# A stretch between two attentions placed as guest steps into one attention of 24 items

## What is computed

```python
# L0: cross attention, 16 heads of 8, adaLN on both sides
x = x + attend(adaln(x) @ Wq, adaln(ctx) @ Wkv) @ Wp
# L1: one head of 128 over the context, then experts
nx = layer_norm(x)
weights = softmax((nx @ Wq) @ (ctx @ Wk).T * 128**-0.5)
evidence = weights @ (ctx @ Wv)
combined = concat(nx, evidence, cond)
probs = softmax(combined @ router_W)                    # 3 experts
routed = sum(probs[e] * (silu(combined @ e_w1[e]) @ e_w2[e]) for e in range(3))
x = x + sigmoid(silu(combined @ gate_w1) @ gate_w2) * (routed @ out_w)
# L2 and L3: self-attention over the 56 tokens, cross attention over the 1500 keys, MLP
x = x + gate_a * (attend(qkv(modulate(ln(x)))) @ W_proj)
x = x + attend(ln(x) @ W_qc, ln(ctx) @ W_kvc) @ W_cproj  # L3: context without the norm
x = x + gate_m * (gelu(modulate(ln(x)) @ W1) @ W2)
```

## Time and profile before

| | us |
|---|---|
| median of 3 runs | 888.12 |
| range of the runs | 883.29 to 888.56 |
| the profiled execution's own time | 883.98 |
| its span | 882.2 |
| first copy of an item's output (L726) | at 89.9 |
| end of a0: last output copy | at 248.96 |
| first output copy of a1 | at 466.97 |
| last output copy | at 857.0 |

### The profile page before, as it was taken

How to read it: one execution, slowest core, us unless ns; L and a number is a source line. 1 busy time by engine, 2 the same in 40 slices (tenths; PEclk the granted TensorE clock), 3 DMA queues, 4 the chain that set the end, 5 groups by cost and what they waited for, 6 DMA issues and landing times.

```text
span 882.2 us, 23060 instructions
## 1 busy us (share of the span) xinstructions
PE 795.9 (90%) x9613; PEld 534.1 (61%) x9613; DVE 593.2 (67%) x1301; ACT 503.2 (57%) x786; POOL 393.2 (45%) x519
## 2 busy tenths in 40 slices
PE   6659999999989988687599999999999899999996
PEld 4336667777656634365167777767766676666763
DVE  7947877777623266454667777876778768777834
ACT  8337777776612220343077776666667656666663
POOL 7764766663000500752856666752335505333000
PEclk9689999999999999898689999999999999999999
DMA  8795545436935200440924454433452443543200
GB/s 213 195 232 124 139 112 141 133 91 199 316 118 161 65 20 1 142 108 15 223 63 130 126 141 125 122 89 108 135 162 83 130 131 89 156 130 97 57 3 10
DMA packets 82171, 106.71 MB, mean 121 GB/s; under 512 B 11502, under 2 KB 75758, under 8 KB 81812
## 3 DMA queue, kind: packets, MB, share of 16 engines
q1 hardware_dynamic: 81492, 104.62, 43.2%
q10 hardware_dynamic: 576, 0.63, 0.3%
HBM read 41.37 MB, written 0.23 MB: 47 GB/s over the span
## 4 chain that ended last, share of the span: by engine, by line
PE 72%; DVE 14%; POOL 6%; ACT 4%; issue 2%; DMA 2%; SPq 0%; DVEq 0%; POOLq 0%; ACTq 0%
PE ring_ps L589 14%; PE oacc_ps L614 14%; PE score_ps L603 12%; PE ring_ps L573 7%; PE ring_ps L566 6%; DVE max_sb L707 4%; PE ring_ps L559 3%; PE ring_ps L1644 2%; DMA kstack<-part_sb 2%; DVE tok L1411 1%; PE score_ps L1491 1%; PE ring_ps L579 1%; POOL hat_sb L773 1%; POOL kstack L2002 1%; ACT prob_sb L686 1%
## 5 line engine op out<-in xcount | busy, mean ns | idle before, releaser
L707 DVE TENSOR_REDUCE max_sb<-ring_ps 128x1 f32<-128x500 f32 x576 | 365.9, 672 | 104.0 <-PE ring_ps L589 101.6
L686 ACT ACTIVATE prob_sb<-score_ps 125x896 f32<-125x896 f32 x288 | 255.3, 921 | 85.3 <-PE score_ps L603 84.7
L589 PE MATMUL ring_ps<-kstack,qstack 128*128 128x500 bf16 x576 | 200.4, 391 | 25.9 <-DMA kstack<-part_sb 11.1
L782 POOL TENSOR_TENSOR key_sb<-key_sb,part_sb 128x500 f32<-128x500 f32 x72 | 82.0, 1140 | 189.5 <-ACT key_sb L668 188.9
L603 PEld LDWEIGHTS score_ps<-qstack,kstack 128*128 128x128 bf16 (+1 forms) x2304 | 139.2, 102 | 42.8 <-issue 11.7
L603 PE MATMUL score_ps<-qstack,kstack 128*128 128x112 bf16 (+1 forms) x2304 | 158.2, 215 | 3.1 <-ACT prob_sb L686 2.3
L614 PE MATMUL oacc_ps<-prob_sb,val_sb 125*32 125x168 f32 (+1 forms) x3456 | 139.5, 294 | 0.9 <-ACT prob_sb L686 0.6
L614 PEld LDWEIGHTS oacc_ps<-prob_sb,val_sb 125*32 125x32 f32 x3456 | 97.5, 109 | 49.0 <-issue 19.6
L589 PEld LDWEIGHTS ring_ps<-kstack,qstack 128*128 128x128 bf16 x576 | 51.1, 99 | 90.3 <-DVE max_sb L707 33.6
L787 POOL TENSOR_TENSOR part_sb<-key_sb,part_sb 128x500 bf16<-128x500 f32 x72 | 82.5, 1146 | 5.6
L773 POOL TENSOR_SCALAR hat_sb<-nat_sb,norm_now 125x128 f32<-125x128 f32 x184 | 81.4, 459 | 1.7
(11 more groups left out here) (301 smaller groups left out, 1003.2 us busy)
## 6 DMA issues: line engine op xcount, KB each, us to landing
kstack<-part_sb SPq DMA_DIRECT2D x432, 125.0 KB, 2.4
nat_sb<-ctx_nat SPq DMA_DIRECT2D x20, 672.0 KB
qstack<-qpart_sb SPq DMA_DIRECT2D x60, 112.0 KB, 2.3
nat_sb<-ctx_T SPq DMA_DIRECT2D x8, 750.0 KB, 4.4
w_sb<-ctx_nat SPq DMA_DIRECT2D x5, 672.0 KB
w_sb<-weights SPq DMA_DIRECT2D x1, 3268.5 KB, 13.5
kstack<-ctx_T SPq DMA_DIRECT2D x4, 750.0 KB, 13.7
nat_sb<-ctx_nat SPq DMA_DIRECT2D x20, 78.0 KB
```

The source lines that it names most:

```text
L589: last = pe.matmul(ps[:, 0:KB], queries(p, n, D), kstack[:, u, p, j * KB:(j + 1) * KB], start=True, stop=True)
L686: return act.activation(dst, score_ps[0:CK, c % 2, :, 0:HALF], ACT.Exp)
L707: return dve.tensor_reduce(max_sb[:, p, j:j + 1], ring_ps[:, self.bank[f"{i}.{name}"], 0:KB], AX.X, ALU.max)
L782: return pool.tensor_tensor(rest, rest, part_sb[:, 0, cols], ALU.subtract)
```

## The change

There is one `Attention`, "att", of 24 items (L0, L2, L3 with 8 each). The stretch is gone. A new class `First`, derived from `Half`, does for one half what the stretch did: its HEAD steps (L0's projection, all of L1) and then the own part that `Half` already had (L2's self-attention, projection and cross queries). Guest e0a (batches 0 to 3) stands in periods 4 to 6, e0b in periods 8 to 10, each with its last steps of GpSimd and SyncE in the period after (e0b's of VectorE, too). L2's items 8 to 15 follow item 7 with no break, so items 8 and 12 wait for the queries that e0a and e0b make. A guest `pre` (class `Before`) has the modulation products (period 0), the load of the weights of L1 and L2 (3076.5 KB, SyncE, period 3) and the anchor products (TensorE, period 3, behind S1). The third layer group's guests move by 8 periods: e2a to 12 to 14, e2b to 16 to 18, e3a and e3b to 21 to 24. `keep_busy` fillers of the stretch, `Dense` d1, d2 and d_mid, `Evidence` and `Own` are removed; `L2_W_proj` has one block of 128 columns instead of four.

The evidence is computed for two batches at a time, in thirds of 500 keys. The context for it is no longer held whole: it comes through two buffers `ev_in`, in twelve steps c0 to c11 per half, each of two transfers of 250 KB; step c(i) waits for the TensorE step that used c(i-2). The scores are copied by ScalarE into `ev_sc`.

```diff
+GUESTS = {'e0a': {...
+         ('pe', 4): 'proj:M0.2 e.mean:K0 e.var:PV0 e.rep:K1 eq:S5 eqk:M1.2 s00:M1.3 s01:PV2 s02:M1.7 pt00:PV4 pt01:PV4 '
+                    'u00:M2.7 pt02:M2.7 u01:M2.7 u02:MTb s10:V2 ut0:V2',
...
+         ('sp', 5): 'c5:load c6:load c7:load c8:load c9:load c10:load c11:s0.0',
...
-        d1 = Dense("d1", [("proj", "dve", "x"), *L.ln_products("ln"), ("q", "dve", "q"), ("qk", "dve", "qk")],
-                   [], ["x", *L.ln_values("ln"), "nx", "q", "qk", "anchors"])
-        evi = Evidence()
...
-        own2 = Own("own2", w("L2_W_qkv", 0, 256, 128), vec("L2_b_qkv", 2))
...
-        a0 = Attention("att0", [(layer0, n) for n in range(B)], EARLY_L0, {})
-        a1 = Attention("att1", [(l, n) for l in (layer2, layer3) for n in range(B)], EARLY_L2,
-                       {B: next_queries(halves[0]), B + HB: next_queries(halves[1])}, halves, BANKS)
...
+        guests = [before, e0a, e0b, e2a, e2b, e3a, e3b]
+        a0 = Attention("att", [(l, n) for l in (layer0, layer2, layer3) for n in range(B)], EARLY_L0,
+                       {B + HB * i: next_queries(g) for i, g in enumerate((e0a, e0b, e2a, e2b))}, guests, BANKS)
...
+                ps = self.ring(pe, "anch")
+                pe.wait_ge(loaded_w1, 16)
+                for k in range(len(ANCHORED)):
+                    last = pe.matmul(ps[:, k * B:(k + 1) * B], anchored(k, 2), cond_sb[:, :], start=True, stop=True)
+                yield self.done("pe", last, "anch")
...
+                w1 = W_AT["L1_Wq"][0]
+                sp.wait_ge(stats_kept, B)
+                sp.dma_start(w_sb[:, w1:W_L3], weights[:, w1:W_L3]).then_inc(loaded_w1, 16)
+                yield "w1"
...
+            HEAD = {
+                "pe": "proj e.mean e.var e.rep eq eqk s00 s01 s02 pt00 pt01 u00 pt02 u01 u02 s10 ut0 s11 s12 pt10 pt11 u10 pt12 "
+                      "u11 u12 ut1 ev lA lB w0 g2 w1 o0 w2 o1 o2 out",
...
+                "dve": "e.x e.xc e.sq e.vs e.xh nx eqk mx0 rec0 sc0 out0 mx1 rec1 sc1 out1 l01 l2 gu m01 m d gh s01 s r pp "
+                       "u0 g u1 h0 h1 u2 x0 h2 x1 a1 x2 a2 outg x",
...
+            def evidence_scores(self, pe, k, j):
...
+                block, loaded = self.part(k, j)
+                pe.wait_ge(*loaded)
+                for t in range(2):
+                    at = (2 * k + t) * LQ
+                    last = pe.matmul(ps[64 * t:64 * t + 64, 0:KB], ev_q[:, at:at + 64], block[:, t, 0:KB], start=True, stop=True,
+                                     skip_group_check=True)
...
+            def combined(self, pe, name, ks):
+                ps = self.ring(pe, name)
+                for i, k in enumerate(ks):
+                    for c, rhs in enumerate((self.xe, self.ev)):
+                        last = pe.matmul(ps[:, i * HT:(i + 1) * HT], anchored(k, c), rhs, start=(c == 0), stop=(c == 1))
...
+            def head_sync(self, sp):
+                for index in range(12):
+                    k, i = divmod(index, 6)
+                    block, (into, _) = self.part(k, i)
+                    if index >= 2:
+                        sp.wait_ge(*self.after("pe", self.taken_in(index - 2)))
...
+                    for t in range(2):
+                        n = HB * self.h + 2 * k + t
+                        if i < NJ:
+                            sp.dma_start(block[:, t, 0:KB], ctx_T[n][:, i * KB:(i + 1) * KB]).then_inc(into, 16)
+                        else:
+                            c = 4 * (i - NJ)
+                            sp.dma_start(block[0:CK, t, :].rearrange("p (c k) -> p c k", c=4), ctx_nat[n][:, c:c + 4, :])\
+                                .then_inc(into, 16)
+                    yield f"c{index}"
```

More of the change, by code:

```diff
@@ new lines @@
+GUESTS = {'e0a': {('act', 4): 'eq:E5 c00:K2 c01:K2 c02:E7 ex0:V0 p00:E11 p01:E11 p02:E11 c10:V2 c11:V2',
[40 rows of a table added]
+         ('dve', 11): 'm.vs:O m.xh:O m.q:O m.q.0:O',
[54 rows of a table added]
+         ('dve', 23): 'e.xc:O e.sq:OTT e.vs:OTT e.xh:OTT e.scaled:OTT e.shifted:OTT',
+         ('dve', 24): 'in0:OTT in1:OTT h0:OTT h1:OTT gated:OTT x:OTT',
+         ('pe', 22): 'proj:PV5 e.mean:MTb',
+         ('pe', 23): 'e.var:S4 e.rep:S10 u0:PV5',
+         ('pe', 24): 'u1:OT y:OTT',
+         ('pool', 21): 'e.rs:k2.2',
+         ('sp', 21): 'store:s2.2'},
+ 'e3b': {('act', 23): 'u0:E11 u1:E11 sq0:E11 u2:E11 u3:E11 sq1:E11 t0:E11 t1:E11 y:E11',
+         ('dve', 24): 'e.x:OTT e.xc:OTT e.sq:OTT e.vs:OTT e.xh:OTT e.scaled:OTT e.shifted:OTT in0:OTT in1:OTT h0:OTT '
+                      'h1:OTT gated:OTT x:OTT',
+         ('pe', 24): 'proj:OTT e.mean:OTT e.var:OTT e.rep:OTT u0:OTT u1:OTT y:OTT',
+         ('pool', 21): 'e.rs:k2.2',
+         ('sp', 21): 'store:s2.2'},
+ 'pre': {('dve', 0): 'mods:M0.1 scales:M0.1',
+         ('dve', 3): 'anch:M0.1',
+         ('pe', 0): 'mods:S1',
+         ('pe', 3): 'anch:S1',
+         ('pool', 0): 'keys0:norm keys1:hat0 pads0:hat0 pads1:hat2 ones:hat2',
+         ('sp', 3): 'w1:load'}}
@@ L1068, in vector, with head_vector @@
             def vector(self, dve):
-                nm, l, h = self.nm, self.layer, self.h
+                yield from self.head_vector(dve)
+                if self.follow:
+                    yield from self.own_vector(dve)
+            def head_vector(self, dve):
+                nm, l = self.nm, self.layer
                 dve.wait_ge(*self.after("pe", "proj"))
@@ L1142, in scalar, with head_scalar @@
             def scalar(self, act):
+                yield from self.head_scalar(act)
+                if self.follow:
+                    yield from self.own_scalar(act)
+            def head_scalar(self, act):
                 nm = self.nm
@@ L1171, in scalar @@
                 act.wait_ge(*self.after("pe", "val"))
-                act.wait_ge(own_pads_ready, 3)
+                act.wait_ge(*before.after("pool", "ones"))
                 for n in range(HB):
@@ L1242, in sync @@
                     return
+                yield from self.head_sync(sp)
                 def placed(part, into):
@@ L1949, in _ @@
             sp.dma_start(x_t, x_T).then_inc(loaded_x, 16)
-            for g in halves:
+            for g in guests:
                 g.begin("sp", sp)
@@ L2130, in _ @@
-            a1.run("pe", pe, -1, only=lambda name: name[0] in "VM")
-            for p in a1.periods():
-                a1.run("pe", pe, p)
         @block.scalar
         def _(act):
-            for g in halves:
+            for g in guests:
                 g.begin("act", act)
@@ L2288, in _ @@
-            d = d2
-            dve.wait_ge(d.pe.sem, d.pe.after("ev"))
-            d.step(dve, dve.tensor_copy(ev_t, d.ps("ev")), "ev")
-            for e in range(E_N):
-                dve.wait_ge(d.pe.sem, d.pe.after(f"l{e}"))
-                d.step(dve, dve.tensor_tensor(by_batch(logit[e]), by_batch(d.ps(f"l{e}")), anchor(e), ALU.add), f"l{e}")
-            d.step(dve, dve.tensor_tensor(xc_t, logit[0], logit[1], ALU.max), "m01")
-            d.step(dve, dve.tensor_tensor(xc_t, xc_t, logit[2], ALU.max), "m")
@@ L2331, in _ @@
-            d.gated(dve, T(8), "L2.gate_a", "y")
-            d.ln_dve(dve, "ln", 1e-6)
-            dve.wait_ge(d.pe.sem, d.pe.after("q"))
-            d.step(dve, dve.tensor_scalar(q_t, d.ps("q"), vec(nm["q_b"]), HD ** -0.5, ALU.add, ALU.mult), "q")
-            d.split(dve, q_t, [qsplit_sb[:, i, :] for i in range(3)], "q")
-            for p in a1.periods(-1):
-                a1.run("dve", dve, p)
 def kernel(**inputs):
```

1045 lines of the change are left out of this document (416 added, 629 removed), and 138 rows, old and new, of tables (EARLY_L2, GUESTS, HEAD, WEIGHTS).

## The result

The changed kernel takes 910.09 us (median of 4 runs, 907.10 to 912.49), the kernel before 885.70 in the same comparison: a ratio of 1.0273, 95% interval 1.0240 to 1.0307. It is slower by 2.7%. The forecast was 860 and its range ended at 894, so neither the size nor the sign held.

The account below looks back on a forecast made before the run. TensorE bounds plain attention periods; the stretch between attentions is a dependent chain. Base 701.7, work 88.0 and 5.2, waits 5, 15, 10, 27 and 6 give a span of 857.9; plus 1.8, 860 us. Range 822 to 894.

Parts of the forecast that it names:

- e0a: First new half, periods 4 to 7: 44.0 us of TensorE work, and a wait of 8 us at its end.
- e0b: Second new half, periods 8 to 11: 44.0 us of TensorE work, and a wait of 16 us at its end.
- e2a: Guest half of the third layer group, there already: keeps its cost inside the base, 94.5 us for three periods.
- Evidence loads: New halves: TensorE waits for context steps, about 6 us at the first half's c5; 10 in all, 3 to 25.
- Rival B: Evidence transfers of 125 partitions run on 5 of 16 engines, 8 us more per half: 876 us, chance 0.22.
- The clock: Half clock behind waits: 3 us at the anchor products in period 3 and 3 after the end of the halves.
- TensorE's work: Head 29.2 and own part 14.8 us per half come back into the attention's periods: 88.0 for both halves.
- Modulation products: They move into period 0 and cost TensorE 2.8 us.
- Anchors: Period 3, behind S1: TensorE waits 12 us for the weight load, plus 3 for the clock: 15, 9 to 16.
- Half ends: Before M0.0 of periods 7 and 11: waits for queries of 8 and 16 us, 3 for the clock: 27, 17 to 33.
- VectorE's burst: M1.2 to M2.4 of periods 5 and 9: 25 guest steps make TensorE wait 3 us per half, 6 in all.
- Rival C: The evidence steps run on still fewer engines, such as three: 902 us, slower than before, chance 0.07.

Follow-up runs that it names:

- the split: The changed kernel with each 125-partition evidence transfer made two, of 112 and 13 partitions: 892.47 us, ratio 1.0090 to the kernel before.
- the reverse edit: The 868.51 us kernel with its evidence transfers whole again, 125 partitions each: 887.87 us, ratio 1.0045 to the kernel before.
- the fastest kernel: Changed kernel with evidence transfers divided, anchor and modulation products moved later, fillers ahead of items 8 and 12, c5 and c6 issued earlier: 868.51 us, ratio 0.9840.
- the fillers' periods: Periods 7 and 11 of the changed kernel with filler matmuls ahead of items 8 and 12: 907.24 us, ratio 1.0196 to the kernel before.

## Why the prediction was wrong

- **The base** (701.7 us) held as far as the table can show it: the items follow one another, and outside periods 4 to 11 the differences sum to 8.3 us.
- **Evidence loads, 10 us (wait 3): the step that failed most.** That its upper bound of 25 is what was measured is luck: it stood for twelve late landings at full width. The forecast took a 125-partition transfer to be as wide as the 128-row ones; it is a third as wide. The waits were 25.4; the split gave 17.6 us back, the reverse edit cost 19.4. Rival B had the mechanism and the price (16), and a chance of 0.22 where the rule and the 112 and 13 partitions in the natural-layout loads of before spoke for it. Its price fits in part by luck: B charged six uncovered steps, and eight waited. What B missed is that everything else in the queue has its share on the five engines, too.
- **The clock, 6 us.** I priced a wait at half clock twice (3 us at the anchors, 3 at one half end). In fact ten stretches at half clock lie in periods 4 to 11, nine of them at or just behind waits of 1.8 to 7.8 us, and they cost 19.7 us of speed where 3 were priced: two thirds of the 28 us of busy time above 194.2 + 88. Not all of it is paid: fillers in all long waits gave TensorE 17 us back, and the time fell by 4 to 9.
- **TensorE's work, 88 us (the step "work that comes back").** Without the lost speed it is 96.6 in the change, 10% more than priced; the fastest kernel gives the same (312.5 busy us, less 15.2 of fillers, 194.2 plain and 7.4 for the half clock: 96). By the lines of that kernel the evidence takes 35.7 us where 29.6 were priced, and the head's 64 dense products 32.4 where 26.2 were, 0.5 each in place of 0.41. Both prices came from rows with many like products in a row; that they cost more one by one between other products is argued, not tried.
- **Modulation products, 2.8 us.** Right at full clock (2.95), but they stood where the clock was at half, and cost 5.2. The memory sets, put at nothing as lying in the removed stretch, stood behind them on GpSimd, which waited 8.8 us.
- **Anchors, 15 us:** right; the weights landed 11.8 us after their issue (the 9 us of pure transfer in its lower bound stand in no row; at the 312 KB per us that the forecast takes elsewhere they are 9.9), period 3 was 1.6 us shorter than priced, and moving the products gave 9.8.
- **Half ends, 27 us:** waits of 6.8 and 7.8 at M0.0 with 2.7 in the chain ahead of it (mean, variance, query), and 4.6 of clock by the fillers' periods: 22, a little less than priced. From the end of V2 to M0.0 e0b's chain took 13.5 us in place of 16.
- **VectorE's burst, 6 us:** TensorE waited 4.7 us there (1.5 at the gate product, the rest at experts, where 1.0 is put down to ScalarE, and the M product behind them, both halves). Nearly right.
- **e2a, no term:** 5.7 us longer than before in the change, at a clock of 0.89 in its third period; in the trace of the fastest kernel it isn't (30.9, 37.5, 26.7). The third period takes 28.9 to 31.5 in all other traces of changed kernels but one (26.6), so this differs between executions; why is open.

Rival C's sign came true, but not its mechanism: the transfers ran on five engines, not three or four. The transfers (17.6) and the under-priced work (9) alone lead from 860 to 886.6, level with the kernel before. Of what remains to 910 the runs point to two terms, the clock (4 to 9) and the place of the modulation products with the memory sets (1 to 4), neither of them clear of the noise by its time; the rest, small waits and e2a's periods, they leave open.
